# The first steps and the last step but one of a hand-scheduled graph kernel, written in another order

## The reference

```python
x = layernorm(x + attention(x, adj))   # 12 heads of 32; scores + beta*adj, masked where adj is 0
x = layernorm(x + digcn(x, adj))       # two layers:
#   a = softmax(h h^T / sqrt(384)) * adj, rows divided by their sum (+1e-10)
#   ctx = upper(a) @ (h Wl^T + bl) + diag(a) * (h Ws^T + bs) + lower(a) @ (h Wr^T + br)
#   h = relu(layernorm(ctx) * g + b)
```

## Time and profile before

| | us |
|---|---|
| median of 3 timed runs | 1298.93 (1297.71 to 1299.69) |
| the profiled execution, its own time | 1300.92 |
| its span on the core | 1299.2 |
| PE busy | 1265.1 |
| DVE busy | 986.1 |
| ACT busy | 630.1 |
| POOL busy | 368.3 |

### The profile page before, as it was taken

How to read it: one execution, slowest core, us unless ns; L and a number is a source line. 1 busy time by engine, 2 the same in 40 slices (tenths; PEclk the granted TensorE clock), 3 DMA queues, 4 the chain that set the end, 5 groups by cost and what they waited for, 6 DMA issues and landing times.

```text
span 1299.2 us, 34507 instructions
## 1 busy us (share of the span) xinstructions
PE 1265.1 (97%) x13844; PEld 1171.7 (90%) x13844; DVE 986.1 (76%) x2672; ACT 630.1 (48%) x1329; POOL 368.3 (28%) x398
## 2 busy tenths in 40 slices
PE   8899999999999999999999999999999999999885
PEld 8899999999999999999999999999999999999774
DVE  5667787777787777787777787777787777787765
ACT  5535545445545445545445545445544445544432
POOL 4222323223323223233223233223233223232211
PEclk9899999999999999999999999999999999999997
DMA  7211110111110111110111110111100111100000
GB/s 252 97 44 57 57 42 16 57 57 57 57 32 27 56 57 57 57 30 29 56 57 56 57 29 30 56 57 57 57 27 31 57 57 57 57 26 20 26 13 25
DMA packets 54174, 66.32 MB, mean 51 GB/s; under 512 B 17792, under 2 KB 40704, under 8 KB 53888
## 3 DMA queue, kind: packets, MB, share of 16 engines
q1 hardware_dynamic: 54016, 64.12, 16.2%
HBM read 38.54 MB, written 12.58 MB: 39 GB/s over the span
## 4 chain that ended last, share of the span: by engine, by line
PE 95%; DVE 1%; DMA 1%; issue 1%; ACT 0%; SPq 0%; POOL 0%; POOLq 0%; ACTq 0%; DVEq 0%
PE bank L355 24%; PE bank L357 23%; PE bank L356 23%; PE bank L545 7%; PE bank L494 4%; PE bank L457 4%; PE bank L442 3%; PE bank L423 3%; PE bank L470 2%; PE bank L480 2%; PE bank L525 1%; DMA late<-in_w 1%; DVE ln_six L1008 0%; POOL ln_rstd L1192 0%; SPq L295 0%
## 5 line engine op out<-in xcount | busy, mean ns | idle before, releaser
L355 PE MATMUL bank<-w_hi,hT_hi 128*128 128x384 f32 x1158 | 405.4, 350 | 0.9 <-DVE hT_lo L933 0.9
L357 PE MATMUL bank<-w_hi,hT_lo 128*128 128x384 f32 x1158 | 390.7, 337 | 0.0
L356 PE MATMUL bank<-w_lo,hT_hi 128*128 128x384 f32 x1158 | 390.6, 337 | 0.0
L355 PEld LDWEIGHTS bank<-w_hi,hT_hi 128*128 128x128 f32 x1158 | 218.7, 189 | 5.4 <-issue 1.1
L356 PEld LDWEIGHTS bank<-w_lo,hT_hi 128*128 128x128 f32 x1158 | 219.3, 189 | 0.0
L357 PEld LDWEIGHTS bank<-w_hi,hT_lo 128*128 128x128 f32 x1158 | 218.7, 189 | 0.0
L962 DVE TENSOR_TENSOR hlr<-bank,rows 128x384 f32<-128x384 f32 x256 | 142.3, 557 | 79.3 <-PE bank L357 76.2
L1192 POOL TENSOR_TENSOR ln_rstd<-ln_var,minus_half 128x2 f32<-128x2 f32 x128 | 98.8, 772 | 349.7 <-DVE ln_var L1014 131.1
L1179 POOL TENSOR_TENSOR probs<-probs,row_max 128x768 f32<-128x768 f32 x64 | 94.5, 1477 | 278.7 <-DVE row_max L902 278.7
L977 DVE TENSOR_TENSOR late<-bank,rows 128x384 f32<-128x384 f32 x128 | 71.4, 558 | 123.6 <-PE bank L357 123.6
L355 PE MATMUL bank<-xT_hi,w_hi 128*128 128x256 f32 x558 | 158.7, 284 | 0.0
(11 more groups left out here) (101 smaller groups left out, 2357.2 us busy)
## 6 DMA issues: line engine op xcount, KB each, us to landing
v_halves<-v_stage SPq DMA_DIRECT2D x128, 99.0 KB, 2.3
xT_in<-in_xT SPq DMA_DIRECT2D x32, 384.0 KB, 3.4
x_in<-in_x SPq DMA_DIRECT2D x32, 384.0 KB, 4.0
out<-late SPq DMA_DIRECT2D x32, 384.0 KB, 2.4
late<-in_w SPq DMA_DIRECT2D x7, 576.0 KB, 6.1
adj_in<-in_adj SPq DMA_DIRECT2D x32, 96.0 KB, 3.9
adjT_in<-in_adjT SPq DMA_DIRECT2D x64, 48.0 KB, 3.2
rows<-in_vectors SPq DMA_DIRECT2D x1, 1536.0 KB, 8.0
```

What stands on the lines that cost most here:

```text
L355: nc.tensor.matmul(o, l_hi, r_hi, start=first and n == 0, stop=False)
L356: nc.tensor.matmul(o, l_hi, r_lo, start=False, stop=False)
L357: done = nc.tensor.matmul(o, l_lo, r_hi, start=False, stop=final and n == last)
```

## The change

At the beginning: ten fp32 matmuls stand for the 20 warm-up transposes. The first two weights come as one array `w_qk`, laid out so that each third of both is one load with 3072 bytes in a row. Unit 0's transposed h goes to banks 5 and 4, and unit 1's scores no longer wait for its copies. ACT splits weight 6 only behind `split_hT`. DVE splits weight 5 behind the norm's shift, and weights 6 and 7 in step 0, behind `max_gram`.

At the end, step 30 gets an order of its own on PE, ACT, DVE and POOL (`next_to_last`): both maxima, shifts and exponentials of unit 31's scores early, its probabilities transposed and its heads made behind the first layer's mix, before z is transposed, and unit 29's last norm in the second half, its `normalize` at the very end of ACT's part. Contexts of the second layer alternate between two tiles with a store semaphore each, and h0 has three slots (`h_slot`).

```diff
--- before.py
+++ after.py
@@ -27,7 +27,7 @@
 STAGES_BEFORE, STAGES_AFTER = 2, 1
-PREWARM = 20
+PREWARM = 10
 NEG = 9000000000000000.0
@@ -53,6 +53,10 @@
+    def h_slot(self, stage):
+        return (self.s + stage) % 3
     def count(self, stage, per, k):
@@ -129,14 +133,15 @@
         c0 = late[:, 2 * D:4 * D].rearrange("p (t d) -> p t d", t=T)
-        c1 = late[:, 4 * D:6 * D].rearrange("p (t d) -> p t d", t=T)
+        c1 = [late[:, at:at + 2 * D].rearrange("p (t d) -> p t d", t=T) for at in (4 * D, 7 * D)]
         self_turned = late[:, 6 * D:7 * D]
-        c = [c0, c1]
...
         RAW = 3
-        RAW_OF = {W_Q: 0, W_K: 1, W_V: 2}
+        RAW_OF = {W_V: 2}
+        qk_raw = late[:, 0:2 * KC * D].rearrange("p (m n k c) -> p m n k c", m=KC, n=2, k=KC)
         w_raw = [late[:, r * KC * D:(r + 1) * KC * D].rearrange("p (k d) -> p k d", k=KC)
@@ -180,6 +185,7 @@
         H_BANKS = [bank[1], bank[2]]
+        FIRST_H_BANKS = [bank[5], bank[4]]
@@ -234,13 +240,20 @@
             sem(n) for n in ("ln2_stats", "ln2_aggr", "ln2_eps", "ln2_rs", "ln2_sh"))
-        y_ready, y_stored = sem("y_ready"), sem("y_stored")
+        y_ready, y_stored = sem("y_ready"), [sem(f"y_stored{i}") for i in range(2)]
+        def context(unit, l):
+            return c0 if l == 0 else c1[unit % 2]
...
             return FIRST_QK_BANKS[unit][m] if unit < 2 else QK_BANKS[m]
+        def h_bank(unit, t):
+            return FIRST_H_BANKS[t] if unit == 0 else H_BANKS[t]
@@ -296,9 +309,7 @@
             for m in range(KC):
-                part = slice(m * P, (m + 1) * P)
-                for n in (W_Q, W_K):
-                    sp.dma_start(w_raw[RAW_OF[n]][:, :, part], w[n][:, :, part]).then_inc(qk_raw_in[m], 16)
+                sp.dma_start(qk_raw[:, m], w_qk[m]).then_inc(qk_raw_in[m], 16)
                 if m == 0:
@@ -338,12 +349,13 @@
                     need(sp, y_ready, st.count(FINAL, 2, 2))
-                    sp.dma_start(out[st.unit(FINAL)], c1).then_inc(y_stored, 16)
+                    sp.dma_start(out[st.unit(FINAL)], context(st.unit(FINAL), 1)).then_inc(y_stored[st.slot(FINAL)], 16)
                 if st.has(EARLY):
...
             steps(step)
-            sp.wait_ge(y_stored, 16 * UNITS)
+            for i in range(2):
+                sp.wait_ge(y_stored[i], 8 * UNITS)
@@ -410,7 +422,8 @@
-                need(pe, hT_ready, st.count(stage - 1, 5, 2))
+                if st.unit(stage) >= 2:
+                    need(pe, hT_ready, st.count(stage - 1, 5, 2))
                 need(pe, o_scaled, st.count(stage - 1, 2, 2))
@@ -550,7 +563,7 @@
             for n in range(PREWARM):
-                nc.tensor.transpose(bank[7][:, 0:P], ident[:, :], ident[:, :])
+                nc.tensor.matmul(bank[7][:, 0:P], ident[:, :], ident[:, :], start=True, stop=True)
             pe.wait_ge(consts_set, 1)
@@ -569,6 +582,25 @@
+            def next_to_last(st):
+                gram(st, 0)
+                project_sides(st, 0)
+                transpose_e(st, 0)
+                project_self(st, 0, 0)
+                project_self(st, 0, 1)
+                mix(st, 0)
+                transpose_probs(st)
+                attend(st)
+                transpose_z(st)
+                gram(st, 1)
+                project_sides(st, 1)
+                transpose_e(st, 1)
+                project_self(st, 1, 0)
+                transpose_h(st)
+                project_self(st, 1, 1)
+                mix(st, 1)
             def step(st):
@@ -618,10 +653,9 @@
                     part = slice(m * P, (m + 1) * P)
-                    act.wait_ge(qk_raw_in[m], 32)
-                    for n in (W_Q, W_K):
-                        nc.scalar.activation(w_hi[:, n, :, part], w_raw[RAW_OF[n]][:, :, part], ACT.Copy
-                                             ).then_inc(wqk_hi_set, 1)
+                    act.wait_ge(qk_raw_in[m], 16)
+                    for i, n in enumerate((W_Q, W_K)):
+                        nc.scalar.activation(w_hi[:, n, :, part], qk_raw[:, m, i], ACT.Copy).then_inc(wqk_hi_set, 1)
@@ -762,13 +800,31 @@
                 take_qk(st, 1)
-                split_weight(6)
                 take_qk(st, 2)
...
                 split_hT(st)
+                split_weight(6)
                 split_weight(7)
                 split_weight(8)
+            def next_to_last(st):
+                exp_gram(st, 0)
+                exp_scores(st, 0)
+                exp_scores(st, 1)
+                scale_self(st, 0)
+                scale_turned(st, 0)
+                take_pT(st)
+                normalize_inner(st)
+                take_zT(st)
+                split_zT(st)
+                exp_gram(st, 1)
+                normalize_h(st)
+                take_hT(st)
+                scale_self(st, 1)
+                split_hT(st)
+                scale_turned(st, 1)
+                normalize_final(st)
@@ -981,12 +1040,12 @@
                 if l == 1:
-                    need(dve, y_stored, st.count(stage - 1, 16, 16))
+                    need(dve, y_stored[st.slot(stage)], st.dma_count(stage - 2))
                 need(dve, ctx_psum, st.count(stage, 4, 2 * l + 1))
...
                 need(dve, self_scaled, st.count(stage, 6, 3 * l + 1))
-                nc.vector.tensor_tensor(c[l][:, 0], CTX_BANKS[l][0][:, 0:D], h_self[:, 0], ALU.add
+                nc.vector.tensor_tensor(context(st.unit(stage), l)[:, 0], CTX_BANKS[l][0][:, 0:D], h_self[:, 0], ALU.add
                                         ).then_inc(ctx_ready[l], 1)
@@ -1049,13 +1110,45 @@
                 heads_out(st)
-                split_weight(5)
                 stats_outer(st)
                 shift(st, MID, ln0_mv, ln0_rstd, ln0_shift, ln0_rs, ln0_sh)
+                split_weight(5)
                 stage_v(st, EARLY)
                 hT_low(st)
-                split_weight(6)
-                split_weight(7)
+            def next_to_last(st):
+                make_ctx(st, FINAL, 1)
+                max_gram(st, 0)
+                mask_scores(st, 0, 4)
+                max_scores(st, 0)
+                max_scores(st, 1)
+                sides_bias(st, 0, 0, LEFT)
+                take_diag(st, 0)
+                sides_bias(st, 0, 0, RIGHT)
+                sides_bias(st, 0, 1, LEFT)
+                sides_bias(st, 0, 1, RIGHT)
+                mask_aT(st, 0)
+                self_bias(st, 0)
+                make_ctx(st, LATE, 0)
+                stats_inner(st, LATE, 0, ln1_den, ln1_stats, ln1_aggr, ln1_eps, ln1_six, ln1_mv, ln1_var)
+                shift(st, LATE, ln1_mv, ln1_rstd, ln1_shift, ln1_rs, ln1_sh)
+                heads_out(st)
+                zT_low(st)
+                max_gram(st, 1)
+                stats_outer(st)
+                sides_bias(st, 1, 0, LEFT)
+                take_diag(st, 1)
+                stats_inner(st, FINAL, 1, ln3_den, ln3_stats, ln3_aggr, ln3_eps, ln3_six, ln3_mv, ln3_var)
+                sides_bias(st, 1, 0, RIGHT)
+                shift(st, MID, ln0_mv, ln0_rstd, ln0_shift, ln0_rs, ln0_sh)
+                final_affine(st)
+                sides_bias(st, 1, 1, LEFT)
+                sides_bias(st, 1, 1, RIGHT)
+                mask_aT(st, 1)
+                final_sum(st)
+                self_bias(st, 1)
+                hT_low(st)
+                shift(st, FINAL, ln2_mv, ln2_rstd, ln2_shift, ln2_rs, ln2_sh)
@@ -1065,10 +1158,16 @@
                     return
+                if st.unit(MID) == UNITS - 1:
+                    next_to_last(st)
+                    return
                 if final:
...
                     max_gram(st, 0)
+                if st.unit(LATE) == 0:
+                    split_weight(6)
+                    split_weight(7)
                 if mid:
@@ -1180,19 +1279,32 @@
+            def next_to_last(st):
+                split_adj(st)
+                shift_scores(st, 0)
+                shift_scores(st, 1)
+                inverse_root(st, LATE, 1, 1, ln1_eps, ln1_var, ln1_rstd, ln1_rs)
+                add_x(st)
+                inverse_root(st, MID, 1, 1, ln0_eps, ln0_var, ln0_rstd, ln0_rs)
+                inverse_root(st, FINAL, 1, 1, ln3_eps, ln3_var, ln3_rstd, ln3_rs)
+                inverse_root(st, FINAL, 1, 1, ln2_eps, ln2_var, ln2_rstd, ln2_rs)
...
+                if st.unit(MID) == UNITS - 1:
+                    next_to_last(st)
+                    return
```

52 lines of the change are left out of this document (32 added, 20 removed).

## The result

The changed kernel takes **1294.29 us** (median of 7 runs, 1292.08 to 1294.9), the kernel before 1299.69 in the same session (7 runs, 1297.71 to 1301.81). The ratio is 0.9954, 95% interval 0.9944 to 0.9964, so 5.4 us or 0.46% faster. The forecast was 1289.8 us with a range from 1286.3 to 1293.8: the sign is right and the gain is 40% less than the 9.1 us forecast. The range began 5.1 us under the 1298.93 that the forecast was taken from, so a gain of 5.4 us lies just inside it; the median itself, beside a kernel before of 1299.69, lies 0.5 us above it. The profiled execution took 1292.08 us with a span of 1290.4, against 1300.92 and 1299.2 before. These two differ by 8.8 us, close to the forecast. Where the other 3.4 us are is the question of this study.

The account below looks back on a forecast made before the run. PE was taken as the bound, busy 1265.1 of 1299.2 us, with idle time and half clock only at the two ends. Start 2.4, middle 6.0 and end 0.7 sum to 9.1 us: 1298.9 to 1289.8 us, range 1286.3 to 1293.8.

Parts of the forecast that it names:

- Rival D: First 50 us: weight 8 lands late, ACT and then PE wait; 1298 us or slower, chance 0.03.
- Rival C: Reordered middle gives its hole and no more, 3.4 us: 1292.4 us, chance 0.1.
- The sign that would have spoken against the forecast: Prediction wrong if steps between 55 and 1210 change length, or PE idles over 1 us between 20 and 50 us.
- (a): Start: one 384 KB load per third of the first weights; first product at 6.5 instead of 7.30, 0.8 us, bounds 0 and 1.2.
- (b): Start: 10 plain fp32 matmuls for 20 transposes, to have PE at 2.4 GHz from about 7.3; 2.4 us with (a).
- 2.4 if the clock is up, 0.5 if not: Start, (a) with (b): 54 products end near 13.0 with early clock, 14.9 if it rises as late as before.
- (c) to (e): Unit 0 to step 0's mix: splits moved, H banks changed, clock kept; mix at 47.15 for 53.14, 6.0 us, bounds 3.4 and 6.5.
- the wait: Middle: unit 1's scores no longer wait for ACT's copies, 0.6 of the 6.0 us.
- The end: Steps 30 and 31: reordering shortens PE's hole before z; 0.7 us with the clock down, bounds -0.5 and 3.1.
- rival B: End: clock kept through the last unit but one, 1.7 us more, 1288.1 us, chance 0.26.
- lower bound of -0.5: End: z comes 0.5 us late and nothing else is won.
- the case with the clock up: End: DVE holds the last gram to 1247.5, its side products to 1248.5 where they stood at 1250.95: 2.4 us.

Follow-up runs that it names:

- the loads alone: Kernel before with only one load per third of the first two weights: 1298.46 us, ratio 0.9992.
- the warm-up alone: Kernel before with only ten plain matmuls in place of the 20 warm-up transposes: 1298.92 us, ratio 0.9994.
- the splits alone: Kernel before with only the three weight splits moved, H banks and the scores' wait as before: 1295.47 us, ratio 0.9972.
- The fillers: Changed kernel with extra matmuls on an unused bank in PE's holes of steps 30 and 31: 1290.02 us, ratio 0.9931.
- DVE's later orders: Changed kernel, later `take_diag`, unit 29's last sum behind hT's low half: 1294.88 us; also unit 30's norm behind z's low half: 1293.14; with fillers: 1292.95.
- the end alone: Kernel before with only `next_to_last`, the context tiles and h0's slots: 1300.82 us, ratio 1.0008.
- all but the end: Changed kernel without step 30's own order, second context tile kept: 1294.54 us, ratio 0.9961 against the kernel before.
- the middle alone: Kernel before with only weight splits moved, unit 0's h in banks 5 and 4, no wait for ACT's copies: 1294.3 us, ratio 0.9963.
- the later `take_diag`: Changed kernel with DVE's `take_diag` of step 30 two places later, behind the third side bias: 1292.82 us, ratio 0.9946.
- DVE's last order: Changed kernel, later `take_diag`, DVE reordered at step 30's end and in the last unit's step: 1293.14 us; with fillers 1292.95 us.

## Why the prediction was right, and where it was off

**The stretches over all profiles.** Each kernel left one profile, and most share stretches with the kernel before or with the changed one (the loads alone and the warm-up alone are left out of the first row, the splits alone out of the second). The fillers and DVE's later orders count for the first two rows only; mean, number of profiles and span in us:

| stretch | old | new | gain | forecast |
|---|---|---|---|---|
| start to unit 0's scores | 15.69 (4, 15.01 to 16.38) | 14.42 (8, 13.70 to 15.90) | 1.3 | 2.4 |
| scores to step 0's mix | 36.37 (4, 35.49 to 36.76) | 31.33 (9, 31.07 to 31.96) | 5.0 | 6.0 |
| gram of step 30 to the end | 85.00 (6, 84.54 to 85.73) | 85.82 (3, 84.78 to 86.68) | -0.8 | 0.7 |

The gains add up to 5.5 us, where the medians show 5.4 and 5.7. The 29 steps between take 1160.42 to 1160.94 us in all fourteen profiles. So the account closes: of the 3.6 us that are missing from the forecast, 1.1 lie in the start, 1.0 in the middle and 1.5 at the end. With so few profiles each gain is known to some tenths only, the last one least.

**Right in its structure.** The gain lies in the first 50 us and is made of what was named: a sooner first product (6.49, forecast 6.5), no hole before h's transposes (31.99, forecast 32.0), the clock kept to the mix (45.20, forecast 44.7), an unchanged run of 29 steps, a 2.00 us hole before z. Rival D (weight 8) did not come: ACT waited 0.17 us for it. Rival C (3.4 us for the middle) is out by the traces: 5.0 us, and a granted clock of 1.00 to the mix. The sign that would have spoken against the forecast, a change of the steps between 55 and 1210, did not show: the 0.40 us of the two profiles lie within what executions differ by.

**(a) and (b), the start.** 0.8 us for the loads holds in every profile that has them: first products between 6.39 and 6.79 in place of 7.28 to 7.52. What was mis-sized is the 1.6 us of clock that (b) gave to the new warm-up: 0.5 is left of it. Products ran at 2.4 GHz from the first in three profiles with the 20 transposes (middle, splits, loads). Some ran at 1.2 GHz in two of five with the transposes (before, the end alone) and in one of nine with the matmuls (all but the end). It varies by execution, and these counts are too few to say that one warm-up is better. The medians don't help: all but the end gained 5.1 us and the middle alone 5.3, each to within some 1.6. A sum that reads "2.4 if the clock is up, 0.5 if not" needed a mean over executions here, as both happen in both kernels.

**(c) to (e), the middle.** Forecast 6.0, measured 5.3 by the median of the middle alone, 5.5 on the pair of traces, 5.0 over all. The parts: the splits 3.8, the banks 1.1 by the trace, of which 0.6 was named as the wait. Of the 1.0 us that is missing, 0.4 comes from the one execution before: from the scores to the mix it took 36.76 us, others with the old order 36.71, 36.52 and 35.49. The rest, 0.6, is the new order, set at 30.77 and measured 31.33: behind h's transposes the side products came after 2.97 us in the profile after, in place of 2.65, and the mix 10.24 us behind these, in place of 10.10.

**The end.** Forecast 0.7, measured between -1.2 (the end alone against before) and +0.7 (with and without it) by the medians, and -0.8 over the profiles, which is under the lower bound of -0.5 that the prediction gave. Two things took the gain. PE's idling before z shrank as forecast, and the clock fell all the same, in both profiles of the changed kernel, so rival B with its 1.7 us did not come there; in the profile with the later `take_diag` it stayed up to 1244 (granted clock 1.00, the gram 0.92 us), so B happens in some executions. The Trainium skill ("TensorE: Matmul & The Clock Gate", A second HAM failure mode) has short idling between groups of matmuls bring the clock to swing. The falls in the profiles of the changed kernel agree with it, with idle pieces of 0.45, 2.00 and 1.41 us. And a wait that was in no step of the prediction took 1.06 us: the change was costed for DVE's queue order but not for POOL's shifts, which it moved to where DVE's `take_diag` runs. The prediction had the means to see it: POOL's `add_x` took 3.11 us beside a DVE split and 2.02 without, and it used this pair for the middle alone. The later `take_diag` takes this wait away. The working of the case with the clock up had a slip as well: its 12.0 us on DVE stand for three terms that add up to 12.6 (6.16, 0.95 and 5.5). It was harmless, since with the clock up and the wait gone the last gram comes 2.6 us earlier (33.48 for 36.07), near the 2.4 it gave.

**The sum.** The change of the span was taken off the median of 1298.93, which the text places 0.3 us under the span. That comparison was a slip: a median of execution times goes with the profiled execution's own 1300.92, and it lies 2.0 us under that. It changed no gain. The larger error is that all durations came from one execution. The mean granted clock of the kernel before is 0.987 to 0.990 from run to run (0.990 in all five runs up to 1298.5 us, 0.987 or 0.988 in the nine from 1298.97 us up, in the first session), the profiled one had 0.988, and the forecast took for the changed kernel the best case at the start. A change that wins clock wins most against an execution that had lost it. The durations of one execution, the clock of (b) and the end with its unforeseen wait are behind the 3.6 us.

## What to carry to other kernels

Where a kernel is one unbroken PE queue, each hole at the ends must be costed twice, as idle time and as clock behind it, and the second over several executions; idle time that can't be removed can be filled with matmuls that nobody reads, which here won 3.9 us beside the 5.4 of the rewriting, though not on top of every order: beside DVE's last order they won nothing that can be told. Before moving work on POOL, list which DVE instructions with two SBUF inputs will run beside it: here two such ones lasted to about the end of POOL's instruction, however small they were. Moving DVE work from ahead of one piece to behind it only moves PE's wait, unless the new place has slack; two of three such moves here made it worse or exchanged one wait for a longer.

## What the runs showed of the hardware that was not expected

- The clock rose during a stretch of transposes alone (3.82 and 3.84 us for 20 in two profiles, 4.53 in another; the last ones 0.11 us apart, the first 0.21). The prediction held the same from the earlier trace rows; these are cleaner, as PE had done nothing before them. The rule in the Trainium skill ("TensorE: Matmul & The Clock Gate", Part 4: PE-mode transpose), by which transposes do not engage the full clock, does not hold here.
- A clock that a warm-up has raised can fall again at once: with the end alone it was back at 1.2 GHz (granted 0.50 from 8 to 10 us) behind 1.87 us of idling and five products at 2.4 GHz. Behind 1.48 to 1.60 us of idling it stayed up in three other profiles.
- The window rows give a granted clock of 1.00 for the first 16 us of nearly all profiles, also where products are 0.21 us apart (before and all but the end). At the start of an execution the spacing of like instructions tells the level, not that column.
- A DVE operation on two numbers per partition took 0.99 us in place of 0.16, up to POOL's end within 0.02 us in two kernels (the changed one and the end alone).
